# Two-layer graph network on one core: a new order for the setup, four PSUM banks under it, and plain float32 for two blocks

## The reference

```
h = layernorm(x + einsum('bnf,nm->bmf', x, adj * adj) + bias)
z_l = h @ W_lang.T;  z_g = h @ W_grav.T;  v = h @ W_V.T
A_l = max(cosine(z_l, z_l), 0) * (1 - eye)
A_g = exp(-dist2(z_g, z_g) / (2 sigma^2)) * (1 - eye)
K = w * rownorm(A_l * adj) + (1 - w) * rownorm(A_g * adj)     # w = sigmoid(gate_logit)
out = layernorm(h + (K @ v) @ W_O.T)
```

## Time and profile before

| | us |
|---|---|
| median of 3 runs | 606.13 (605.9 to 607.47) |
| the profiled execution | 605.54 |
| its span, first to last instruction | 603.7 |
| start of the first projection of group 0, where the setup ends for PE | 44.33 |
| PE busy in the span | 588.5 (97%) |
| mean granted clock of PE, as a share of full | 0.992 |

### The profile page before, as it was taken

How to read it: one execution, slowest core, us unless ns; L and a number is a source line. 1 busy time by engine, 2 the same in 40 slices (tenths; PEclk the granted TensorE clock), 3 DMA queues, 4 the chain that set the end, 5 groups by cost and what they waited for, 6 DMA issues and landing times.

```text
span 603.7 us, 10056 instructions
## 1 busy us (share of the span) xinstructions
PE 588.5 (97%) x3803; PEld 462.4 (77%) x3803; DVE 361.8 (60%) x814; ACT 296.4 (49%) x532; POOL 125.4 (21%) x344
## 2 busy tenths in 40 slices
PE   7999999999999999999999999999999999999992
PEld 6977868688686868778686868868686877868771
DVE  3854383747658373756748374865837375674375
ACT  2753525537363544636363553736354463636423
POOL 0201101222221221222220122222122122222022
PEclk8999999999999999999999999999999999999997
DMA  7903030131304031131304013130303110100003
GB/s 233 271 5 69 1 69 20 57 84 53 88 23 100 19 97 44 53 88 54 71 36 105 20 59 81 54 87 25 99 18 98 44 52 18 54 1 36 35 18 122
DMA packets 20703, 38.68 MB, mean 64 GB/s; under 512 B 2096, under 2 KB 2096, under 8 KB 20656
## 3 DMA queue, kind: packets, MB, share of 16 engines
q1 hardware_dynamic: 20656, 38.05, 22.1%
HBM read 21.27 MB, written 16.78 MB: 63 GB/s over the span
## 4 chain that ended last, share of the span: by engine, by line
PE 96%; DVE 1%; DMA 1%; ACT 1%; SPq 0%; issue 0%; POOL 0%; POOLq 0%
PE ring L367 65%; PE bank_s L384 10%; PE ring L475 5%; PE bank_y L329 3%; PE bank_z L432 2%; PE bank_z L342 2%; PE bank_y L342 2%; PE bank_y L432 2%; PE bank_s L329 2%; PE bank_s L393 1%; DMA yT<-in_L_gnn_W_lang_dram 1%; PE bank_y L405 1%; PE bank_s L412 1%; DVE z_bn L807 0%; DVE h_sb L802 0%
## 5 line engine op out<-in xcount | busy, mean ns | idle before, releaser
L536 ACT ACTIVATE yT<-ring 128x512 f32<-128x512 f32 x128 | 72.5, 591 | 129.0 <-PE ring L367 129.0
L367 PE MATMUL ring<-hT_hi,T_hi 128*128 128x512 f32 x320 | 127.8, 399 | 0.0
L367 PE MATMUL ring<-hT_hi,T_lo 128*128 128x512 f32 x320 | 124.8, 390 | 0.0
L367 PE MATMUL ring<-hT_lo,T_hi 128*128 128x512 f32 x288 | 112.3, 390 | 0.0
L367 PE MATMUL ring<-M_hi,hT_hi 128*128 128x512 f32 x256 | 103.4, 404 | 0.0
L367 PE MATMUL ring<-M_hi,hT_lo 128*128 128x512 f32 x256 | 100.2, 391 | 0.0
L367 PE MATMUL ring<-M_lo,hT_hi 128*128 128x512 f32 x256 | 100.0, 391 | 0.0
L732 DVE TENSOR_TENSOR diag_scr<-P_sb,ident_c 128x512 f32<-128x512 f32 x16 | 11.1, 692 | 140.4 <-ACT P_sb L536 140.4
L367 PEld LDWEIGHTS ring<-hT_hi,T_hi 128*128 128x128 f32 x320 | 60.0, 188 | 23.7 <-issue 12.2
L367 PEld LDWEIGHTS ring<-hT_hi,T_lo 128*128 128x128 f32 x320 | 60.1, 188 | 12.9
L581 ACT ACTIVATE h_sb<-h_sb,z_nb,z_rs 128x512 f32<-128x512 f32 x63 | 51.8, 824 | 23.7 <-POOL z_nb L975 23.7
(11 more groups left out here) (115 smaller groups left out, 851.7 us busy)
## 6 DMA issues: line engine op xcount, KB each, us to landing
out_dram<-h_sb SPq DMA_DIRECT2D x64, 256.0 KB, 2.0
x_sb<-in_x_dram SPq DMA_DIRECT2D x30, 512.0 KB, 6.4
x_sb<-in_x_dram SPq DMA_DIRECT2D x4, 256.0 KB, 5.5
yT<-in_L_gnn_W_lang_dram SPq DMA_DIRECT2D x1, 1024.0 KB, 5.9
yT<-in_L_gnn_W_grav_dram SPq DMA_DIRECT2D x1, 1024.0 KB, 9.1
h_sb<-in_L_gnn_W_O_dram SPq DMA_DIRECT2D x1, 1024.0 KB, 11.2
h_sb<-in_L_gnn_W_V_dram SPq DMA_DIRECT2D x1, 1024.0 KB, 14.5
bias_bc<-in_L_gnn_bias_dram SPq DMA_DIRECT2D x1, 256.0 KB, 6.9
```

Source lines behind the costliest of these rows:

```text
L367: last = pe.matmul(ring[ring_of(g, k)][:, :], a, b, start=n == 0, stop=n == len(terms) - 1)
L536: return act.activation(dst, src, ACT.Copy, scale=scale)
```

## The change

- Loads: W_lang comes first, in four DMAs of 128 rows (256 KB each), each with a semaphore of its own; then adj, W_grav, half of group 0's x, bias, the other half of x, W_V, W_O. SP then waits until W_O has landed before it issues group 1's x and the gate scalars. Each half of group 0's x is one DMA over 128 partitions (`x_0`), and group 0's results are stored in two DMAs per tile (`out_0`).
- `WARM_UP` goes from 27 to 9.
- The setup goes over four banks, `set_bank` = the three of the ring and `bank_s`. So result k waits for result k - 4, where it waited for k - 3. The first projections wait accordingly.
- In each form the last block row (i = 3, 128x128) comes first, and is made straight from the unsplit weights in plain float32: 4 matmuls in place of 12.
- The orders on PE, ACT and DVE are new: `layer0(0, 0)` comes after three results of form L, and group 0's transposes are spread between the turned blocks of W_O and the rows of M. The gate scalars' arithmetic moves to the end of the setup.

The core of the diff (`setup(k)`, `hi_setup(k)` and `lo_setup(k)` handle result k on PE, ACT and DVE; k = 0 to 3 is form L, 4 to 7 form G, 8 to 11 W_O, 12 to 15 M; within a form the order is `ROWS` = 3, 0, 1, 2; lines of the shared bodies of ACT's and DVE's helpers are left out):

```diff
-    WARM_UP = 27
...
+    ROWS = [DC - 1] + list(range(DC - 1))
+    WARM_UP = 9
     NRING = 3
+    NSET = NRING + 1
     NSETUP = 2 * DC + 2 * DC
...
+        set_bank = ring + [bank_s]
...
+                    sp.dma_start(x_sb[g % 2][half(a), :, :], x_v[g][a]).then_inc(done, 16)
+
+            def load_x_0(h):
+                t = slice(2 * h, 2 * h + 2)
+                sp.dma_start(x_sb[0][:, t, :], x_0[:, t, :]).then_inc(x0_loaded[h], 16)
             def load_w(i, w):
                 sp.dma_start(w_raw[i], w.rearrange("(c p) d -> p c d", p=R)).then_inc(w_loaded[i], 16)
-            load_x(0, x0_loaded[0], slice(0, 2))
+            for c in range(DC):
+                sp.dma_start(w_raw[0][:, c, :], w_lang[c * R:(c + 1) * R, :]).then_inc(w0_loaded[c], 16)
             for c in range(2):
                 sp.dma_start(adj_c[half(c), :], adj).then_inc(adj_loaded, 16)
-            load_w(0, w_lang)
+            load_w(1, w_grav)
+            load_x_0(0)
             sp.dma_start(bias_bc[:, :], bias.partition_broadcast(R)).then_inc(bias_loaded, 16)
-            load_x(0, x0_loaded[1], slice(2, 4))
+            load_x_0(1)
+            load_w(2, w_v)
+            load_w(3, w_o)
+            sp.wait_ge(w_loaded[3], 16)
+            load_x(1, x_loaded[1])
             sp.dma_start(gates[:, 0:1], gate_logit.partition_broadcast(R)).then_inc(gates_loaded, 16)
             sp.dma_start(gates[:, 1:2], log_sigma.partition_broadcast(R)).then_inc(gates_loaded, 16)
-            load_w(1, w_grav)
-            load_w(3, w_o)
-            load_w(2, w_v)
-            load_x(1, x_loaded[1])
...
-                    sp.dma_start(out_v[g][p % 2][p // 2], h_sb[g % 3][:, p, :]).then_inc(stored[p], 16)
+                    if g == 0:
+                        for c in range(2):
+                            sp.dma_start(out_0[p // 2][p % 2][c], h_sb[0][half(c), p, :]).then_inc(stored[p], 16)
+                    else:
+                        sp.dma_start(out_v[g][p % 2][p // 2], h_sb[g % 3][:, p, :]).then_inc(stored[p], 16)
             load(2)
...
             def layer0(g, h):
                 if g == 0:
-                    pe.wait_ge(x0_loaded[h], 32)
+                    if h == 0:
+                        pe.wait_ge(mix_steps, 4)
+                    pe.wait_ge(x0_loaded[h], 16)
                 else:
                     pe.wait_ge(x_loaded[g % 2], 32 * ((g + 1) // 2))
...
+                    elif g == 1:
+                        pe.wait_ge(setup_split, NSETUP)
                     if g > 0:
...
                 if g == 0 and k < NRING:
-                    pe.wait_ge(setup_split, NSETUP - NRING + 1 + k)
+                    pe.wait_ge(setup_split, NSETUP - NSET + 1 + k)
                 else:
                     ring_free(place(g, k))
                 if kind == "u":
+                    if g == 0:
+                        pe.wait_ge(setup_split, NSETUP)
                     s = slice(j * R, (j + 1) * R)
                     terms = [(a[:, i, s], b[:, i, :]) for i in range(DC)
...
+            def rows_of_t(s, i):
+
+                terms = [(a[:, e, i * R:(i + 1) * R], b[:, e, i * R:D]) for e in range(DC)
+                         for a, b in parts(W_hi[s], W_lo[s], W_hi[s], W_lo[s])]
+                at = DC * s + ROWS.index(i)
+                if at >= NSET:
+                    pe.wait_ge(setup_split, at - NSET + 1)
+                if i == DC - 1:
+                    own = slice(i * R, D)
+                    for e in range(DC):
+                        if s == L:
+                            pe.wait_ge(w0_loaded[e], 16)
+                        else:
+                            pe.wait_ge(w_loaded[s], 16)
+                        last = pe.matmul(set_bank[at % NSET][:, 0:R], w_raw[s][:, e, own], w_raw[s][:, e, own],
+                                         start=e == 0, stop=e == DC - 1)
+                    last.then_inc(setup_done, 1)
+                    return
...
+                    if i == 0 and n % 3 == 0:
+                        pe.wait_ge(w_lo_done, DC * s + n // 3 + 1)
+                    last = pe.matmul(set_bank[at % NSET][:, 0:D - i * R], a, b, start=n == 0, stop=n == len(terms) - 1)
                 last.then_inc(setup_done, 1)
-                at += 1
+
+            def turn_w_o(e):
+                at = 2 * DC + e
+                if e == 0:
+                    pe.wait_ge(w_loaded[3], 16)
+                pe.wait_ge(setup_split, at - NSET + 1)
+                for f in range(DC):
+                    last = pe.transpose(set_bank[at % NSET][:, f * R:(f + 1) * R], w_raw[3][:, f, e * R:(e + 1) * R],
+                                        ident[:, :])
+                last.then_inc(setup_done, 1)
+
+            def rows_of_m(i):
+                at = 3 * DC + i
+                terms = [(a[:, e, i * R:(i + 1) * R], b[:, e, :]) for e in range(DC)
+                         for a, b in parts(W_hi[2], W_lo[2], W_hi[3], W_lo[3])]
+                if i == 0:
+                    pe.wait_ge(w_lo_done, 3 * DC)
+                pe.wait_ge(setup_split, at - NSET + 1)
+                for n, (a, b) in enumerate(terms):
+                    if i == 0 and n % 3 == 0:
+                        pe.wait_ge(setup_split, 2 * DC + n // 3 + 1)
+                    last = pe.matmul(set_bank[at % NSET][:, :], a, b, start=n == 0, stop=n == len(terms) - 1)
+                last.then_inc(setup_done, 1)
+
+            def setup(k):
+                if k < 2 * DC:
+                    rows_of_t(k // DC, ROWS[k % DC])
+                elif k < 3 * DC:
+                    turn_w_o(k - 2 * DC)
+                else:
+                    rows_of_m(k - 3 * DC)
...
             pe.wait_ge(ident_ready, 2)
             for _ in range(WARM_UP):
                 pe.transpose(bank_s[:, 0:R], ident[:, :], ident[:, :])
...
+            setup(0)
+            setup(1)
+            setup(2)
+            layer0(0, 0)
+            setup(3)
+            setup(4)
+            layer0(0, 1)
+            setup(5)
+            setup(6)
+            setup(7)
+            setup(8)
+            setup(9)
+            transpose_h(0, 0)
+            setup(10)
+            transpose_h(0, 1)
+            setup(11)
+            setup(12)
+            transpose_h(0, 2)
+            setup(13)
+            setup(14)
+            transpose_h(0, 3)
+            setup(15)
...
+            def hi_weight(i, c):
+                if i == 0:
+                    act.wait_ge(w0_loaded[c], 16)
+                elif c == 0:
+                    act.wait_ge(w_loaded[i], 16)
+                copy(W_hi[i][:, c, :], w_raw[i][:, c, :]).then_inc(w_hi_done, 1)
...
+            def hi_setup(k):
+                act.wait_ge(setup_done, k + 1)
+                if k < 2 * DC:
+                    hi_row(k // DC, ROWS[k % DC])
+                else:
+                    copy((W_hi[3] if k < 3 * DC else M_hi)[:, k % DC, :], set_bank[k % NSET][:, :]).then_inc(setup_hi, 1)
...
+            hi_weight(0, 0)
+            hi_weight(0, 1)
+            hi_weight(0, 2)
+            hi_setup(0)
+            hi_weight(0, 3)
+            hi_weight(1, 0)
+            hi_weight(1, 1)
+            hi_setup(1)
+            hi_weight(1, 2)
+            hi_setup(2)
+            hi_weight(1, 3)
+            hi_setup(3)
+            hi_weight(2, 0)
+            hi_weight(2, 1)
+            hi_setup(4)
             normalise_h(0, 0)
+            hi_setup(5)
+            hi_weight(2, 2)
+            hi_weight(2, 3)
+            hi_setup(6)
             normalise_h(0, 1)
-            hi_weight(2)
-            for i in range(DC):
-                hi_row(G, i)
-                if i >= 2:
-                    normalise_h(0, i)
-
-            hi_value(W_hi[3], 2 * DC)
-            for p in range(NP):
-                copy_hT(0, p)
-                hi_hT(0, p)
-            hi_value(M_hi, 3 * DC)
+            hi_setup(7)
+            hi_setup(8)
+            hi_setup(9)
+            copy_hT(0, 0)
+            hi_setup(10)
+            hi_setup(11)
+            normalise_h(0, 2)
+            hi_hT(0, 0)
+            hi_hT(0, 1)
+            hi_hT(0, 2)
+            exp_gates()
+            copy_hT(0, 1)
+            copy_hT(0, 2)
+            normalise_h(0, 3)
+            hi_setup(12)
+            hi_setup(13)
+            hi_setup(14)
+            hi_hT(0, 3)
+            copy_hT(0, 3)
+            hi_setup(15)
...
+            lo_weight(0, 0)
+            lo_weight(0, 1)
+            lo_setup(0)
+            lo_weight(0, 2)
+            blocks_of_ident()
+            lo_weight(0, 3)
+            mixing()
+            lo_weight(1, 0)
+            lo_setup(1)
+            lo_weight(1, 1)
+            lo_weight(1, 2)
+            lo_setup(2)
             add_y(0, 0)
             add_y(0, 1)
-            lo_row(L, 0)
             count_y(0, 0)
-            lo_weight(1, 0, 2)
-            lo_row(L, 1)
-            lo_weight(1, 2, DC)
-            lo_row(L, 2)
-            lo_row(L, 3)
-
-            dve.wait_ge(gate_exp, 1)
```

(72 more changed lines are left out.)

113 lines of the change are left out of this document (47 added, 66 removed).

## The result

The changed kernel takes 600.86 us (median of 4 runs, 600.55 to 601.48) against 606.14 before: a ratio of 0.991, with a 95% interval of 0.9893 to 0.9927. The forecast was 600.9. The profiled executions are closer together than the medians, 601.0 and 605.54, with spans of 599.2 and 603.7.

The account below looks back on a forecast made before the run. PE, busy 588.5 of 603.7 us, was taken as the bound. The first projection at 6.7 + 30.5 + 1.9 = 39.1 against 44.33, 5.2 us earlier, gave a median of 600.9 us; range 599.5 to 603.3.

Parts of the forecast that it names:

- That only the start of the first projection counts: Whole kernel: later steps keep their instructions, so only group 0's first projection start, 44.33 before, matters.
- The sum: Setup on PE: 6.7 + 30.5 + 1.9 puts the first projection at 39.1 against 44.33, 5.2 us earlier.
- The clock: PE in the setup: low clock level until 10.5 (9.8 at best, 12.2 at worst), costing 1.9 us.
- DVE's slack: DVE's low parts of W_O: ready at 28.4, PE asks for the fourth block at 29.0; slack 0.5 us.
- The signs of being wrong: Setup: a late last piece of W_lang, `setup(12)` waiting for `setup_split`, or ACT's `hi_weight(2, 0)` waiting for W_V.
- The landings: Setup loads: W_lang's pieces issued 0.7 apart, each taking 3.5 to 3.7 us, last at 6.2; W_grav at 10.7.
- (d): Loads of W_lang: pieces do not overlap, last lands at 15.5, 9.3 later; 3.8 us slower, 609.9; chance 0.03.
- What must be hidden: Setup beside PE: four banks cost nothing and remove the stall; DVE, POOL, loads and stores must stay behind PE's work.
- (b): Setup: ACT and DVE become the bound, W_grav, x or W_V late; gain 3.3 to 3.8, 602.5; chance 0.13.
- (a): PE's clock in the setup: low level lasts to 13.9, 1.7 us more; gain 3.5, 602.6; chance 0.17.
- (c): PE's clock: rises near 7 to 8.5 as plain matmuls count, DVE sets the end; gain 6 to 6.7, 599.8; chance 0.10.
- (e): Group 0: a new wait takes back the setup's gain, no change beyond 0.3%; gain under 1.8 us; chance 0.04.

Follow-up runs that it names:

- e7: Changed kernel with 27 warm-up transposes, and form L's row 0 taken ahead of W_grav's blocks on ACT and DVE: 600.28 us.
- e3: Changed kernel with the setup over the three banks of the ring, as before, in place of four: 601.32 us.
- e4: Changed kernel with form G made as before: rows in order 0 to 3, all by split matmuls, no plain block: 601.28 us.
- e5: Changed kernel with W_lang loaded by one DMA of 1 MB in place of four of 256 KB: 601.13 us.
- e6: Changed kernel with each half of group 0's x loaded by two DMAs of 64 partitions and one store per tile, as before: 603.57 us.
- e10: Changed kernel with the order of loads of before, W_lang still in four pieces: 604.39 us.
- e2: Changed kernel with the 27 warm-up transposes of before in place of 9: 600.21 us.
- e1: Kernel before with W_lang's load issued ahead of group 0's first half of x and adj: 606.48 us, ratio 0.9997.
- e11: Kernel before with W_lang's load first, then adj, then group 0's x: 605.07 us, ratio 0.9971.

## Why the prediction was right

*That only the start of the first projection counts*: right. In fourteen kernels the rest of the span is 559.3 to 559.8.

*The sum*, 39.1, was 0.5 short of 39.57, and its terms are close. Row 0's start: 6.7, measured 6.81. The clock: a rise at 10.5 and a price of 1.9, measured 10.31 and 1.8. Form G's plain block: 0.9, measured 0.89. Most of the 0.5 is a hold-up by DVE ahead of M's row 0, 0.34 us, which the profile does not list as a wait. It shows when PE's starts are laid beside those of e7, where DVE was earlier. The changed kernel:

```profile
26.61 0.66 PE L520 MATMUL bank_s<-ident,h_sb 128*128 128x128 f32 x4
27.30 0.70 PE L534 MATMUL ring<-W_own,hT_hi 128*128 128x512 f32 x2
```

e7:

```profile
26.13 0.60 PE L520 MATMUL bank_s<-ident,h_sb 128*128 128x128 f32 x4
26.48 0.70 PE L534 MATMUL ring<-W_own,hT_hi 128*128 128x512 f32 x2
```

The same four transposes are followed by M's row 0 after 0.69 us, and after 0.35 in e7. DVE's first low part of W_O was done at 27.15 in the changed kernel. The rest is in groups that come after another kind of matmul: the 12 of 256 columns behind `layer0(0, 0)` took 1.54 us from start to start where the earlier trace rows gave 1.43.

*DVE's slack*, 0.5 us, was reckoned at the fourth block of W_O, and there it was so: low part done at 28.95, asked for at 29.47. But the first block was the tight one, and the prediction did not look at it. Its working is off as well: 14.8 and 13 us make 27.8 and not 28.4. DVE did take 13.1 us, but from 15.84, as W_grav's later landing had put its work back; `layer0(0, 0)` had ended at 14.5. So 28.95 was met within 0.6 us partly by luck.

*The signs of being wrong*: two of the three came, in small. M's row 0 is `setup(12)`, and it was held up by `setup_split`. And ACT's `hi_weight(2, 0)` did wait for W_V, in ACT's timeline:

```profile
17.77 1.15 ACT L600 ACTIVATE hT_hi<-h_sb 128x512 fp32r<-128x512 f32 x2 [1.10 <-DMA h_sb<-in_L_gnn_W_V_dram]
```

Nothing in PE's setup followed from this second wait: W_V had landed at 17.8, inside the 16 to 18 of the prediction, and ACT soon stood idle for another 1.66 us, for POOL. The prediction itself lets W_V land as late as 20 without loss, so this sign was drawn too tight.

*The landings*: right in sum, wrong in their parts. Pieces of 256 KB took 2.6 to 4.2 us and not 3.5 to 3.7, issued 0.46 and not 0.7 apart; the last landed at 6.3 for 6.2. W_grav landed at 11.7 for 10.7. The wait of PE that this could have caused showed only as the 0.34 us above; e3 and e4, whose chains run through that landing, show that DVE's work begins with it. The four pieces do not pay in series: they were there 5.6 us after the first issue, and one DMA of 1 MB in e5 5.6 us after its own. The Trainium skill's fixed part of about 2.0 us for each DMA (DMA: Bandwidth & Descriptors, Anatomy of one DMA) is stated there for DMAs issued from GpSimd, while SP issues these; four of them one after the other, 8.0 us, do not agree with the 5.6. Its rule to batch into at least 1 MiB (the same page, Bandwidth) is what e5 does: 601.13 us and 600.86, no difference. In rival (d), 9.3 us later and 5.2 us gained would be 4.1 us slower, not 3.8.

*What must be hidden*: the fourth bank was put at nothing beyond the old stall, and hid a further 0.5 to 0.9 us in e3's profile. The loads of x I called an advantage only in passing, in rival (b). e6 puts them, with the split stores, at 1.5 to 2.7 us, more than any single part but the load order of e10.

*The medians*: 5.3 us apart, the forecast 5.2, but the profiled pair 4.5. The forecast hit the median better than its own sum deserved, and that is luck: the start moved by 4.76 us where the sum had 5.2, and the 0.7 between medians and profiled pair is noise of the runs.

*Rivals*: (a) did not come (10.31), (b) is close, as e6, e3 and the 0.34 us show, (c)'s early rise came in e2, by transposes and not by the plain matmuls, and was worth only 0.4 because x and DVE were next, (d) is out by the landings, (e) by the rest of the span.

## What to carry to other kernels

Where the matmul engine is busy for 97%, price a new setup by one event, the start of the steady state, and sum PE's work from the moment when its first operand can be there. Moving a load forward gives little or nothing while any operand that the orders ask for earlier stands behind it (0 in e1, 1.0 to 1.8 us in e11): after each such move, ask which landing is next. Before removing a wait, look at how far behind the next engine is: 1.2 us of clock came down to 0.4. Work out an engine's slack at every block that is asked for, the first above all, and look for short hold-ups in the starts of instructions, as the list of waits can miss them.

## What the runs showed of the hardware

- Loads into 64 partitions went with slow neighbours, in one execution: in e6 W_grav landed at 13.3, 1.6 us or more later than in the six kernels that issue it at the same time, and in the stretch in which its half loads of x were under way (10.68 to 17.51) 217 GB/s moved at a DMA share of 1.06, and in the next 374 at 1.04.
- A small load waits with the large ones issued before it: the second DMA of adj, 16 KB, took 3.5 us behind four pieces of W_lang, and 7.3 behind W_lang and x (e1).
- Float32 transposes alone can be followed by the rise of PE's clock: in e2 its record at the full level begins at 4.45, after nothing but transposes since 1.51. The moment is not the kernel's alone: with the same 27 transposes first it came at 4.45 (e2), 5.3 (e1, e7), 7.06 (before) and 7.13 (e11), and with the same nine transposes and four pieces at 5.28 (e4), 9.33 (e3), 10.31 (after) and 10.68 (e6), where rows 0 and 1 of form L took 5.57 to 6.97 us. The start of the steady state moved by much less (e2: 5.9 us of rise, 0.4 of start), since another engine or a load was always near.
